# Unread unit products added on TensorE ahead of the first conditioning products and in its early waits

## What is computed

```
y = x @ W[subject_id].T + b[subject_id]              # conditioning, a 256x256 matrix per sequence
q, k, v = projections of y, 16 heads of 16
sim = q k^T / 4 / (|temperature| + 0.1)
scores = sum over 5 frequencies f of alpha * sin(2 pi sim / f + phi)
w = sigmoid(scores); w = w / (sum(w) + 1e-10)
x = x + layernorm((w v) @ Wo.T + bo)
z = layernorm(x + relu(x @ W1[lang] + b1) @ W2[lang] + b2), scaled and shifted by lang
c = 32 steps (over the sequences) of c = sigmoid(..) * c + sigmoid(..) * tanh(..), each from z and c
out = x + tanh(z @ wo.T + c_final @ uo.T + bo)
```

## Time and profile before

| what | value |
| --- | --- |
| median of 3 executions | 325.21 us (322.84 to 325.45) |
| the profiled execution, own time | 326.03 us |
| its span | 324.2 us |
| mean granted TensorE clock | 0.989 |
| busy TensorE, VectorE, ScalarE, GpSimd | 285.8, 274.5, 255.6, 52.1 us |

### The profile page before, as it was taken

The page is one execution under the profiler, slowest core; times in us unless marked ns, Lnnn a source line. Parts: engine busy times, 40 slices in busy tenths (PEclk is TensorE's granted clock), DMA queues, the critical chain, the costliest instruction groups (busy, mean ns, idle before and its releaser), DMA issues.

```text
span 324.2 us, 7389 instructions
## 1 busy us (share of the span) xinstructions
PE 285.8 (88%) x2695; PEld 177.5 (55%) x2695; DVE 274.5 (85%) x600; ACT 255.6 (79%) x374; POOL 52.1 (16%) x58
## 2 busy tenths in 40 slices
PE   0797898786979998999999999999999999998871
PEld 0476647673646855645567646556664546543350
DVE  3058999999889999999999999999998999554266
ACT  1049999998999999999999999999998695412123
POOL 5000120003030013411100233330012412210000
PEclk9999999998999999999999999999999999999997
DMA  6487834556462256056333140702222362020007
GB/s 176 137 261 255 314 60 108 127 140 176 84 173 62 31 148 128 0 126 170 50 81 93 42 68 1 149 16 67 43 68 32 65 141 50 3 33 2 0 2 256
DMA packets 32374, 31.97 MB, mean 99 GB/s; under 512 B 10706, under 2 KB 24274, under 8 KB 32338
## 3 DMA queue, kind: packets, MB, share of 16 engines
q1 hardware_dynamic: 27410, 26.67, 29.7%
q0 software_dynamic: 4352, 4.20, 8.5%
q10 hardware_dynamic: 576, 0.64, 0.8%
HBM read 23.36 MB, written 2.10 MB: 79 GB/s over the span
## 4 chain that ended last, share of the span: by engine, by line
PE 27%; DVE 26%; ACT 22%; issue 10%; SPq 5%; DMA 4%; POOL 4%; DVEq 0%; ACTq 0%; POOLq 0%
DVE sc L1624 7%; PE pg L694 6%; ACT ang L1140 5%; ACT ang L1131 5%; PE pg L685 5%; DVE ang L1613 3%; DMA wc<-in_cond 3%; ACT sc L1150 2%; POOL rs L409 2%; PE pf L491 2%; PE pf L513 2%; DVE ang L1604 2%; PE pav L589 2%; PE pf L571 2%; POOL rs L406 2%
## 5 line engine op out<-in xcount | busy, mean ns | idle before, releaser
L1140 ACT ACTIVATE ang<-ang,qs 128x2560 f32<-128x2560 int32 x32 | 77.3, 2428 | 0.3 <-DVE ang L1613 0.2
L1624 DVE SCALAR_TENSOR_TENSOR sc<-ang,ratio,sc 128x512 f32<-128x512 f32 (+1 forms) x120 | 73.1, 635 | 0.4
L1131 ACT ACTIVATE ang<-sc,phase 128x512 int32<-128x512 f32 (+1 forms) x108 | 63.2, 648 | 0.0
L685 PE MATMUL pg<-gate_w,zT 128*64 128x384 f32 x256 | 50.5, 498 | 0.4 <-DVE zT L1749 0.2
L694 PE MATMUL pg<-gate_u,cT 128*64 128x384 f32 x256 | 47.5, 492 | 1.5 <-DVE cT L1768 1.4
L1613 DVE TENSOR_SCALAR ang<-ang 128x2560 int32<-128x2560 int32 x32 | 47.5, 1484 | 0.1
L1180 ACT ACTIVATE gat<-pg 128x384 f32<-128x384 f32 x32 | 15.6, 486 | 26.9 <-PE pg L694 26.7
L1604 DVE TENSOR_SCALAR ang<-sc,phase 128x256 int32<-128x256 f32 (+1 forms) x92 | 33.6, 411 | 2.3 <-ACT sc L1122 2.2
L513 PE MATMUL pf<-wc,xg 128*64 128x256 f32 x128 | 18.4, 436 | 12.0 <-DMA wc<-in_cond 10.8
L694 PEld LDWEIGHTS pg<-gate_u,cT 128*64 128x64 f32 x256 | 17.0, 136 | 21.6 <-issue 15.1
L685 PEld LDWEIGHTS pg<-gate_w,zT 128*64 128x64 f32 x256 | 15.6, 136 | 18.7 <-issue 16.4
(11 more groups left out here) (114 smaller groups left out, 477.6 us busy)
## 6 DMA issues: line engine op xcount, KB each, us to landing
wc<-in_cond SPq DMA_DIRECT2D x30, 257.0 KB, 3.2
w<-in_up SPq DMA_DIRECT2D x32, 128.5 KB, 2.7
wa<-in_down SPq DMA_DIRECT2D x32, 66.0 KB, 2.3
xt<-in_xt SPq DMA_DIRECT2D x8, 256.0 KB, 3.1
xt<-rows POOLq DMA_DIRECT2D x8, 256.0 KB, 4.1
w<-x POOLq DMA_DIRECT2D x8, 256.0 KB, 4.0
xg<-in_x SPq DMA_DIRECT2D x3, 512.0 KB, 4.7
qm<-qT SPq DMA_DIRECT2D x48, 32.0 KB, 2.1
```

Of the source, the lines that this page charges most:

```text
L685: pe.matmul(pg[n % 2][u * L:(u + 1) * L, 0:GCOLS], zT[:, q % 2, kc, t * L:(t + 1) * L], gate_w[:, kc, u, :], start=False, stop=(kc == KC - ...
L1131: op = act.activation(ang[:, n % SLOTS, f, r], unit(n)[:, r], ACT.Identity, scale=TURN / FREQS[f], bias=phase[:, p * NF + f:p * NF + f + 1])
L1140: act.activation(a.bitcast(F32), a, ACT.Sin, scale=2 * PI_LOW / TURN, bias=qs[:, 3:4]).then_inc(sine_ready, 1)
L1624: op = dve.scalar_tensor_tensor(out=unit(n)[:, r], in0=ang[:, n % SLOTS, f, r].bitcast(F32), scalar=ratio[:, p * NF + f:p * NF + f + 1], i ...
```

## The change

Twenty-two unit products are put between the wait for `eye` and the first conditioning products. Two are put ahead of `turn_tokens(0)` and two behind it. The four places around `scores(0)` and `scores(1)` get four in place of three. Around the third group's conditioning, two are put ahead of `turn_residual(0)`, and two places with four get three. Nothing else is changed; the queues, waits and semaphores stay as they are.

```diff
             pe.wait_ge(eye_s, 16)
             pe.wait_ge(eye_s, 16)
+            warm(22)
             condition(0, 0)
             condition(0, 1)
+            warm(2)
             turn_tokens(0)
+            warm(2)
             queries(0, 0)
             keys(0, 0)
-            warm(3)
+            warm(4)
             scores(0)
-            warm(3)
+            warm(4)
             queries(0, 1)
             keys(0, 1)
-            warm(3)
+            warm(4)
             scores(1)
-            warm(3)
+            warm(4)
             values(0, 0)
             values(0, 1)
             warm(4)
...
             condition(3, 1)
             condition(4, 0)
             condition(4, 1)
+            warm(2)
             turn_residual(0)
-            warm(4)
+            warm(3)
             adapter_down(0)
             turn_tokens(2)
             adapter_up(0)
             queries(2, 0)
             keys(2, 0)
-            warm(4)
+            warm(3)
             queries(2, 1)
             turn_normed(0)
             keys(2, 1)
```

## The result

Medians: 324.1 us before (4 executions, 322.84 to 325.45) and 320.67 us after (4, 319.97 to 322.28). The ratio is 0.9884, 95% interval 0.984 to 0.9928: 1.2% faster, where 0.7% was forecast and the range ended at 320.8. The profiled execution took 320.5 us, 5.5 us less than that of before.

A forecast was written before the change was run, and what follows sets the result against it. The start was taken as a single file with TensorE at 1.2 GHz. A 2.87 us gain there less 0.6 us at 80 us gave 2.3 us: 322.9 us from a median of 325.21, 0.7% less, range 320.8 to 325.9.

The forecast's parts named there:

- The single file: Up to the first scores each engine waits for the one before; a microsecond out is a microsecond off the end.
- The start's sum: Up to the first scores: 1.45 us delay against faster conditioning, turns, queries to scores, and scores; 2.87 us gained.
- 5.0 us of work: TensorE's start: clock rises after 5.0 us of continuous work, at 7.7 us, so the 22 products end at 10.0 us.
- the cost at 80 us: Two products ahead of `turn_residual(0)` have no cover, as ScalarE's copy waits for TensorE: 0 to +0.85 us, taken as +0.6.
- the slow stretch at 78.4 to 81.8 us: Third group's conditioning and turns stay slow behind 2.29 us of idleness; at full clock they would gain 1.5 us more.
- The small additions: Products near the start, around turns and scores: hidden in waits, costed at nothing; 0.1 to 0.4 us if uncovered.
- ended in a gap: Against the no-gain rival (13%, 325.0 us): the 3.69 us of conditioning ended in a gap, the products have none.
- its rival with 18%: Larger gain, 18%: clock rises after 4.1 us (0.45 us more), stretch at 78.4 us not slow (1.5 more); 321.0 us.
- The size against the span: Skill's ramp penalty under 1% of a typical span, gain at most 3.25 us; the rows' four terms give 4.3 us (1.3%).

The follow-up runs named there:

- 80 us alone: The three edits at 80 us (two products ahead of `turn_residual(0)`, three for four in two places) on the kernel before: 324.75 beside 324.26 us, ratio 1.0005.
- 12 products: The change with 12 products in place of 22 ahead of the first conditioning, measured twice: 322.08 us (0.9911) and 321.89 us (0.9916).
- 44: The change with 44 products in place of 22 ahead of the first conditioning: 328.47 us, ratio to before 1.011.
- eight products on the kernel before: The kernel before with eight products between `condition(3, 1)` and `condition(4, 0)`, ahead of the DMA wait at 75 us: 324.22 beside 324.26 us, ratio 0.9993.

## Why the prediction was right and wrong

**The single file, right.** That the start is a file in which each microsecond counts, that its work ran at half clock although the granted clock read 1.00, and that the gain is carried to the end: where the clock did not fall, the time between is the same within 1.1 us for starts from 16.2 to 20.75 us.

**The start's sum, right in the mean.** It said 2.87 us, with products ending at 10.0 us and first scores near 17.2. The five profiles with the whole start (the change and those without the edits at 80 us) have first scores at 16.70 to 17.91 us, mean 17.39; the three with the old start (before, 80 us alone, and 20.28 us in the run that only fills the wait at 75 us) 20.01 to 20.75, mean 20.35: 2.96 us. About 0.3 us of that is the matrices, which landed later in the other two (conditioning from 8.83 and 9.30 us) than in the profile of before (8.56) that the sum was made from. In the profile on record the rise came after 3.2 in place of 5.0 us of work, which let the products end at 9.4 in place of 10.0 us. That was luck for the profiled pair; the other four took 7.34 to 7.89 us for the 44 passes, that is 4.6 to 5.7 us to the rise by the same working. So 5.0 was a fair middle and no constant.

**The steps that failed.** The sum was 2.87 - 0.6 = 2.3 us, and the ratios of three measurements average 3.6 us. Two of its terms were wrong.

The first is the cost at 80 us. "So there is no cover" left out what stands next in TensorE's list: `adapter_down(0)` with a DMA of its own. 0.6 us was charged. The wait ahead of ScalarE's copy did grow by 0.5 us, but the stretch that the two products are in went from 2.62 and 2.86 us to 2.82 us, and the time between in the table from a mean of 288.47 to one of 288.66 us, 0.2 us. The times show no difference (0.9914 with, 0.9916 without), though they could not show one of 0.6. Where the weights are there in time the forecast's half microsecond is real. With this term at nothing the sum would have been 2.87 us, 322.3 us or a ratio of 0.991; measured were 0.9884, 0.9866 and 0.9914.

The second was put at nothing: the slow stretch at 78.4 to 81.8 us was taken to stay as it is, since "the same 2.29 us of idleness stands ahead of it". It is no fixed wait. It was 0.77 to 2.72 us from profile to profile, 1.72 to 1.85 in the five with the whole start, and the clock fell there in none of these. Over all executions the lower mean clock is 5 of 20 with the change and 67 of 112 before, at 2.1 to 2.2 us each: an estimate of 0.7 to 0.8 us.

**The small additions, right for the sum, wrong as a reading.** They were costed at nothing as hidden and were thought idle. Without the 22 they bring 0.8% themselves (0.9922), most of it through the two gaps they fill (0.9942 with these alone). The forecast had even noted that conditioning "ended in a gap" as the reason that it did not raise the clock, and did not draw the conclusion. The parts do not add: 0.9940 and 0.9922 would give 0.986 together, the change was measured at 0.9884, 0.9866 and 0.9914, because both raise the same clock and it rises once.

**What is left.** The three measurements of the change average 0.989, or 3.6 us. 2.96 us of it is the start, which the experiments show. The other 0.6 us is within the intervals, and the smaller share of executions with the lower clock is what the record offers for it. The forecast kept the stretch at full clock as a part of its rival with 18%. But this part is argued and not shown: where the clock was low is known of the profiled executions only, filling that wait on the kernel before changed nothing (0.9993), and why 18 of 24 executions have the lower clock with the 22 alone and 5 of 20 with the whole change is open. The 5.5 us between the two profiled executions are 3.3 us of start (20.01 to 16.70) and 2.2 us of the time between (290.91 to 288.68).

**The size against the span.** The Trainium skill ("TensorE: Matmul & The Clock Gate", Part 1) has the ramp's penalty under 1% of a typical span. The rows had 4.3 us (1.3%) for this kernel; the start that the change got back is 2.96 us (0.9%), so no run here measured more than 1% for the ramp alone. The same part says that the number of slow products differs from run to run, and the profiles now show it: the 44 passes had 3.2 to 5.7 us to the rise.

## What to carry to other kernels

Where TensorE starts cold in a serial stage, look at the pace of its passes and at the gaps between its calls: fill gaps under a microsecond behind real work first (four unread products brought 0.6% here), and add products ahead of it only as many as the wait covers at the lower clock. Products that outlast the wait cost their full time. Before charging an added product to an engine that waits, read what else is queued ahead of that engine's next need, its DMAs too. And before taking a wait for a DMA as given, look at it in more than one profile: here it was 0.8 to 2.7 us, and each fall of the clock behind it came with one of the long ones.

## What the runs showed of the hardware

The clock rose 3.2 to 5.7 us after gapless work began, in the five profiles with the whole start; with gaps of 0.78 and 0.89 us in the work it had not risen after 11 us (three profiles). Once up, gaps of that size left it up in the profiles of the 22 products alone. At 75 us it fell in five of the six profiles with a wait of 2.29 us or more, and in none of the nine with one of 1.93 us or less. The wait's length is not all of it: 2.72 us brought no fall, and with 12 products the clock still read 1.00 for the first 0.9 us of the work behind the wait (74.16 to 75.08 us) and 0.50 behind that. At the end of the kernel it fell in the changed kernel's profile at 306 us, behind waits of 1.38 and 0.38 us only, and likewise in three others (80 us alone, 44, eight products on the kernel before). The granted clock reads 1.00 from the start to the first rise, where the pace is that of half speed.
